# Taps and decays of a long convolution: four block buffers, loaded three blocks ahead

## The chip, the cores and the metric

One core of a Trainium2 chip. The metric is the time of one execution on the device in microseconds, the median of three runs. The core has TensorE (PE; its weight loads are shown as PEld), VectorE (DVE), ScalarE (ACT), GpSimd (POOL) and SyncE (SP), which run their own instruction streams and wait for each other by semaphores. Transfers are issued into queues by SP, ACT and POOL and carried by 16 DMA engines.

## What is computed

Two residual layers over x of shape 8 x 4096 x 512 in float32. The first is a layer norm, a causal convolution along the 4096 positions with a kernel of its own for each of the 512 channels (a sum of 16 decaying exponentials), and a scaled copy; the second is a mixture of 8 low-rank experts, of which each token takes two. Cut to the core:

```python
x = x + conv(layernorm(x))     # k[d,l] = sum_n p*beta*gamma*scale * q[d,n]**l, plus omega*input
x = x + experts(layernorm(x))  # y = w * (gelu(x @ A1.T @ B1) @ A2.T @ B2), for 4096 tokens
```

The experts' layer has as many tokens as one sequence has positions here (4096 of 32768), so it touches an eighth of the rows.

## The kernel before

The 4096 positions of a sequence are cut into 32 chunks of 128. A chunk's rows lie on the 128 partitions, 8 sequences x 32 chunks = 256 chunks lie along the free side. The work is done in two halves of four sequences (g = 0 and g = 1), and between them stands the experts' layer. I call g = 0 the first layer and g = 1 the last one, by their place in time.

A half is cut into four tiles of 128 channels (`DG` = 4, t = 0 to 7 over both halves), each of 128 x 128 x 128 floats, which is 8.39 MB; a tile into 8 blocks of 16 channels (`BT` = 8), and a block into two units of 8 channels. `xb` holds two tiles, one in each half of it: while tile t is computed in one, tile t-1 is stored from the other and then tile t+1 loaded into it. Each of these is cut into 16 pieces of 512 KB (`PIECES`).

The convolution inside a chunk is a product with a 128 x 128 Toeplitz matrix of taps for each channel; what goes from chunk to chunk is a scan. A unit is made of: centring by the mean, one half of the channels on POOL (L512) and the other on DVE (L1137); scaling on DVE (L1148); the chunks' sums into the states on PE (L1333, with `near`); the shift of the states on ACT (L859) and the scan on DVE (L1174); the local product on PE (L1346, with `wb`) and what the carried states add (L1358); and the addition to x on DVE (L1158).

The Toeplitz matrices of a block are made on chip from its taps. The taps (256 KB) and decays (128 KB) of all 32 blocks are written to HBM at the start and are then loaded, block by block, in both halves. `taps_in` holds the taps of two blocks, block i on partitions 32(i%2) to 32(i%2)+31. ACT turns them into `wb` (`reverse`, L878 and L879, two calls for a block) and copies half of the matrix (`lower`, L885). POOL copies the decays from `dk` to `near` (`place_decays`, L482). `wb` and `near` hold two blocks.

What sets the order of the transfers is SP's instruction stream. For each block of a tile (b = 0 to 7) `tile` issues `load_weights` for the next block (taps L683, decays L686), then at b = 0 waits until the tile before is wholly added (`s_ev`), and then issues its share of the 32 pieces, 4 or 5 in a step: first the 16 stores of tile t-1 (L638 and L641), then the 16 loads of tile t+1 (L618). A load of piece j waits for the store of that piece by a running count. The first tile of a half has nothing to store, the last nothing to load. `load_weights(i, h)` waits until the taps and decays of block i-2 have been turned and placed, and until all decays before have landed; all this is in SP's order, so that what stands behind a wait waits too. `centre` on POOL and DVE waits for all pieces of x of its tile (`s_x`).

The first two blocks are loaded from ACT's queue (L837, L838), while the rows of x stream in for the statistics. POOL's `centres` is written out in Python for g = 0 (all indices constants); for g = 1 it runs in a hardware loop with indices in registers, except at the first and last block of each tile.

Of the kernel before, what the change touches and what calls it, by code (L numbers as in the profile page):

```python
# [48 lines left out]
def build(nc, x, delta, alpha, beta, gamma, omega, ew, ei, w1a, w1b, w2a, w2b, out, ei_experts=8):  # L49
# [20 lines left out]
    TB = 4  # L70
    NL = P // LR
# [35 lines left out]
    with ctx:  # L107
# [17 lines left out]
        dk = sb("dk", [P, 2, N * KD])  # L125
# [125 lines left out]
        s_dk = sem("s_dk")  # L251
# [9 lines left out]
        s_w = [sem(f"s_wk{k}") for k in range(2)]  # L261
# [13 lines left out]
        s_out = sem("s_out")  # L275
        s_first = sem("s_first")
# [110 lines left out]
        def _(pool):  # L387
# [85 lines left out]
            def place_decays(i):  # L473

                h = i % 2
                if not isinstance(i, int):
                    h = pool.snap(h)
                dst = near[:, bass.ds(h, 1)].rearrange("p h s z n -> p (h s) z n")[:, :, 0:3:2, :]
                src = dk[:, bass.ds(h, 1)].rearrange("p h (n s d) -> p (h s) d n", s=SB, d=2)
# [22 lines left out]
            def centres(g):  # L502
                def centre(i, first, final):
                    for k in range(2):
                        u = 2 * i + k
                        if k == 0 and tile_start(i, g):
                            place_decays(i)
                        if not (g == 0 and isinstance(i, int) and i < BT):
                            wait(pool, s_x, tiles_in(i, g))
                        wait(pool, s_xn, u - 1)  # L510
                        wait(pool, s_st, u - 1)
                        pool.tensor_tensor(cen[:, k, 0:UC // 2].rearrange("p d r -> p r d"),  # L512
                                           unit_view(pool, g, i, k)[:, :, 0:UC // 2],
                                           mean[:, g * P:(g + 1) * P][:, :, None].to_broadcast([P, P, UC // 2]),
                                           ALU.subtract).then_inc(s_cen, 1)
                        if g == 1 and first and k == 0:
                            scatter(NQ - 1, 0)
                        if k == 0 and not tile_start(i, g) and not (g == 1 and first):
                            place_decays(i)
                        if g == 0 and first and k == 1:  # L520
                            clear(1)
                        if g == 0 and SENT + u < NSEND:
                            send(SENT + u)
                if g == 0:
                    for i in range(NK):
                        centre(i, i == 0, i == NK - 1)
                else:
                    over_tile_blocks(pool, g, lambda i, begin, end: centre(i, isinstance(i, int) and i == NK, end))
# [55 lines left out]
            pool.wait_ge(s_first, 16 * YP * DG)  # L584
# [19 lines left out]
        def _(sp):  # L604
# [18 lines left out]
            def stored(g, t):  # L623

                def until(j):
                    if g == 1:
                        return 0, 16 * (PIECES - YP) * (DG - 1) + 16 * PIECES * (t - DG) + 16 * (j + 1)
                    if j < YP:
                        return 16 * YP * t + 16 * (j + 1), 0
                    return 0, 16 * (PIECES - YP) * t + 16 * (j + 1 - YP)  # L630
                return until

            def store_tile(g, t, pieces):

                for j in pieces:
                    r0, row, d0 = piece(g, t, j)
                    if g == 0 and j < YP:
                        sp.dma_start(y_rows[:, j * PR:(j + 1) * PR, bass.ds(d0, P)],  # L638
                                     xb_row[:, bass.ds(r0, PR), :]).then_inc(s_first, 16)
                    else:  # L640
                        sp.dma_start(o_rows[:, bass.ds(row, PR), bass.ds(d0, P)],  # L641
                                     xb_row[:, bass.ds(r0, PR), :]).then_inc(s_out, 16)
# [29 lines left out]
            def load_weights(i, h):  # L672
# [10 lines left out]
                sp.dma_start(taps_in[h * ZR:(h + 1) * ZR], src).then_inc(s_w[h], 16)  # L683
                wait(sp, s_wd, placed)
                wait(sp, s_dk, kept)
                sp.dma_start(dk[:, h, :], dec).then_inc(s_dk, 16)  # L686

            def tile(g, t, first, final):
                for b in range(BT):
                    if not (first and b == 0) and not (final and b == BT - 1):  # L690
                        load_weights(t * BT + b + 1, (b + 1) % 2)
# [11 lines left out]
                    if final and g == 0 and b >= BT // 2:  # L703
                        if b == BT // 2:
                            sp.wait_ge(s_out, 16 * (PIECES - YP) * t)
                            sp.wait_ge(s_first, 16 * YP * t)
# [61 lines left out]
            load_weights(NK, 0)  # L768
            load_weights(NK + 1, 1)
# [11 lines left out]
            sp.wait_ge(s_out, 16 * (PIECES - YP) * (DG - 1) + 16 * PIECES * DG)  # L781

        @block.scalar
        def _(act):
# [48 lines left out]
            for h in range(2):  # L833
                row = taps_d[h:h + 1].rearrange("k s i d -> k (s i d)")
                src = bass.AP(row.tensor, row.offset, [[2, ZR], [2 * (P + ZR), SB], [1, 2 * P]])
                wait(act, s_dk, 16 * h)
                act.dma_start(taps_in[h * ZR:(h + 1) * ZR], src).then_inc(s_w[h], 16)  # L837
                act.dma_start(dk[:, h, :], decay_d[h:h + 1].rearrange("k s n d -> (k s) (n d)")).then_inc(s_dk, 16)  # L838
# [6 lines left out]
            def steps(i, h, first, final):  # L845
                for k in range(2):
# [18 lines left out]
                    if not final:  # L865
                        reverse(i + 1, k, 1 - h)
# [5 lines left out]
            def reverse(i, k, h):  # L872

                dst = wb[:, h, k * QB:(k + 1) * QB]
                src = taps_in[h * ZR:(h + 1) * ZR, k * QB:(k + 1) * QB].rearrange("p s (m d) -> p s d m", d=2)[:, :, :, ::-1]
                wait(act, s_w[h], 16 * (i // 2 + 1))
# [18 lines left out]
            def over_parities(g):  # L895
# [12 lines left out]
            over_parities(0)  # L908
# [63 lines left out]
            over_parities(1)  # L972
# [541 lines left out]
```

## Time and profile before

| | |
|---|---|
| median of three runs | 1257.15 us (1255.29 to 1258.32) |
| profiled execution | 1263.37 us, its span 1261.3 us |
| busy PE / DVE / ACT / POOL | 76% / 72% / 67% / 49% of the span |
| moved | 287.88 MB, 228 GB/s over the span |
| first half of the convolution (g = 0) | about 128 to 431 us |
| experts' layer | about 431 to 925 us |
| last half (g = 1) | about 925 to 1230 us, then its last stores |

The profile is of one execution. Its shares of busy time are means over stages that differ, so the stages are read one by one. A DMA share is the mean busy share of the 16 DMA engines, counted over their packets; it can be a little over 1. In a wait, "A <- B" says that A sat idle and that B released it; a wait for several things is put down to the one that came last. A "q" behind an engine (SPq) is its queue of transfers and registers.

### The profile page before, as it was taken

The numbers are of one execution on the slowest core, as the hardware profiler recorded it, in microseconds if no ns is written. First come the engines' busy times: TensorE is split into PE (matmuls) and PEld (weight loads), VectorE is DVE, ScalarE is ACT, GpSimd is POOL, SyncE is SP. The second block draws the span as 40 slices with busy tenths as digits, with TensorE's granted clock in tenths as the row PEclk, the third lists the DMA queues.
The fourth block names the chain that finished last, engine by engine and source line by source line (L and its number), as shares of the span: only waits on it lengthen the run. The fifth ranks groups of instructions, "written<-read, shape, count | busy, mean of one in ns | idle before, by whom it ended". The sixth has DMA issues, their size and how long they took to land.

```text
span 1261.3 us, 34527 instructions
## 1 busy us (share of the span) xinstructions
PE 954.1 (76%) x11452; PEld 770.1 (61%) x11452; DVE 909.8 (72%) x1495; ACT 842.9 (67%) x1191; POOL 617.4 (49%) x755
## 2 busy tenths in 40 slices
PE   3740787768778849999999899998978776776780
PEld 2520676656666736777777677776756665665660
DVE  6978898758769527777777777775469885775880
ACT  4841787758668726767766667667678776675870
POOL 4142886647545126666766666665553232231320
PEclk9975899889879969999999999999989898887995
DMA  7998957979979899999998898884368599898909
GB/s 247 326 387 293 226 132 207 273 178 288 272 193 282 275 280 278 261 252 267 238 226 232 200 226 229 228 200 107 82 155 187 141 286 233 228 267 182 283 17 266
DMA packets 337535, 287.88 MB, mean 228 GB/s; under 512 B 18088, under 2 KB 285000, under 8 KB 336962
## 3 DMA queue, kind: packets, MB, share of 16 engines
q1 hardware_dynamic: 293698, 212.01, 61.3%
q0 software_dynamic: 19520, 36.26, 14.7%
q10 hardware_dynamic: 24256, 38.81, 9.2%
q8 instruction: 37, 0.61, 0.2%
q14 instruction: 24, 0.20, 0.1%
HBM read 197.41 MB, written 100.61 MB: 236 GB/s over the span
## 4 chain that ended last, share of the span: by engine, by line
PE 27%; SPq 20%; DMA 12%; issue 11%; DVE 8%; ACT 2%; POOL 1%; POOLq 1%; DVEq 1%; ACTq 0%
SPq L641 8%; PE ps L1440 7%; DMA wide<-y_d,pick_g 7%; SPq L618 7%; PE ps L1453 6%; DMA wide<-taps_d 4%; PE ps L1346 3%; SPq L683 3%; DVE xb L1158 3%; PE ps L1358 2%; PE ps L1413 2%; PE ps L1465 2%; PE ps L1425 2%; PE ps L1333 2%; SPq L686 1%
## 5 line engine op out<-in xcount | busy, mean ns | idle before, releaser
L1346 PE MATMUL ps<-xn,wb 128*128 128x128 f32 x2048 | 294.1, 303 | 46.5 <-ACT wb L885 46.4
L1346 PEld LDWEIGHTS ps<-xn,wb 128*128 128x128 f32 x2048 | 268.1, 211 | 65.7 <-ACT wb L885 51.2
L512 POOL TENSOR_TENSOR cen<-xb,mean 128x512 f32<-128x512 f32 x128 | 142.2, 1111 | 270.3 <-DVE state L1174 218.5
L951 ACT ACTIVATE cen<-ps 128x1024 f32<-128x1024 f32 x156 | 155.9, 1021 | 136.5 <-PE ps L1440 120.4
L1148 DVE TENSOR_TENSOR xn<-cen,rstd 128x1024 f32<-128x1024 f32 x128 | 171.5, 1340 | 58.2 <-POOL cen L512 43.3
L878 ACT ACTIVATE wb<-wide 32x1024 f32<-32x1024 f32 x128 | 145.9, 1140 | 88.5 <-DMA wide<-taps_d 71.0
L1333 PE MATMUL ps<-xn,near 128*32 128x128 f32 x2048 | 89.8, 297 | 146.2 <-DVE xn L1148 75.4
L1440 PE MATMUL ps<-carry,wb 64*128 64x256 f32 x1248 | 169.9, 402 | 26.6 <-DVE carry L1221 26.3
L1158 DVE TENSOR_TENSOR xb<-xb,ps 128x1024 f32 (+1 forms) x128 | 152.8, 1194 | 14.0 <-PE ps L1358 13.8
L1453 PE MATMUL ps<-cen,xn 128*64 128x128 f32 x2496 | 161.1, 277 | 0.9 <-ACT cen L951 0.8
L1453 PEld LDWEIGHTS ps<-cen,xn 128*64 128x64 f32 x2496 | 136.7, 137 | 39.7 <-ACT cen L951 19.9
L1333 PEld LDWEIGHTS ps<-xn,near 128*32 128x32 f32 x2048 | 53.6, 115 | 170.0 <-issue 96.8
L493 POOL DMA_INDIRECT out<-carry,pick_s x78 | 126.4, 1621 | 56.0 <-issue 40.4
L1440 PEld LDWEIGHTS ps<-carry,wb 64*128 64x128 f32 x1248 | 113.6, 189 | 57.1 <-issue 44.7
L1137 DVE TENSOR_TENSOR cen<-xb,mean 128x512 f32<-128x512 f32 x128 | 137.5, 1074 | 0.0
L879 ACT ACTIVATE wb<-wide 32x768 f32<-32x768 f32 x128 | 116.3, 909 | 1.5
L1202 DVE BATCH_NORM_STATS2 tstat<-wide 128x6 f32<-128x512 f32 x78 | 53.7, 692 | 84.5 <-DMA wide<-y_d,pick_g 78.6
L561 POOL COPY xn<-xb 128x256 f32 x156 | 83.8, 583 | 58.3 <-PE ps L1453 57.3
L544 POOL DMA_INDIRECT wide<-y_d,pick_g x78 | 84.7, 1086 | 48.1 <-POOL pick_g L541 36.2
L459 POOL DMA_INDIRECT slot_d<-rowf,posi x64 | 100.3, 1567 | 11.0 <-issue 10.6
L1358 PE MATMUL ps<-state,carry 32*128 32x128 f32 x2048 | 96.9, 305 | 0.1
L1174 DVE TENSOR_TENSOR_SCAN state<-carry,shift_s 128x128 f32<-128x128 f32 x128 | 51.6, 403 | 60.0 <-ACT shift_s L859 59.8
(164 smaller groups left out, 1352.7 us busy)
## 6 DMA issues: line engine op xcount, KB each, us to landing
out<-xb SPq DMA_DIRECT2D x116, 512.0 KB
xb<-L_attn_x SPq DMA_DIRECT2D x96, 512.0 KB
xb<-L_attn_x SPq DMA_DIRECT2D x32, 1024.0 KB, 9.7
xb<-L_attn_x ACTq DMA_DIRECT2D x128, 256.0 KB
wb<-L_ffn_w_B SPq DMA_DIRECT2D x78, 256.0 KB
wide<-taps_d SPq DMA_DIRECT2D x62, 256.0 KB
y_d<-xb SPq DMA_DIRECT2D x16, 512.0 KB
dk<-decay_d SPq DMA_DIRECT2D x62, 128.0 KB
```

What stands on the lines that cost most here:

```text
L493: pool.indirect_dma_start(out=o_tok[0:T], out_offset=bass.IndirectOffsetOnAxis(ap=pick_s[:, 2 * k + h:2 * k + h + 1], axis=0), in_=route_o ...
L512: pool.tensor_tensor(cen[:, k, 0:UC // 2].rearrange("p d r -> p r d"), unit_view(pool, g, i, k)[:, :, 0:UC // 2], mean[:, g * P:(g + 1) * ...
L878: act.activation(dst[0:ZR], src, ACT.Copy)
L951: act.activation(act_h[:, b % 2].rearrange("p f t -> p (f t)"), ps[:, 2 * (b % 2):2 * (b % 2) + 2, :].rearrange("p a t -> p (a t)"), ACT.G ...
L1137: dve.tensor_tensor(cen[:, k, UC // 2:].rearrange("p d r -> p r d"), unit_view(dve, g, i, k)[:, :, UC // 2:], mean[:, g * P:(g + 1) * P][: ...
L1148: dve.tensor_tensor(xn[:, k], cen[:, k], rstd[:, g * P:(g + 1) * P][:, None, :].to_broadcast([P, UC, P]), ALU.mult).then_inc(s_xn, 1)
L1158: dve.tensor_tensor(view, view, ps[:, QB * k:QB * k + QB, 0:2 * P] .rearrange("p b (d r) -> p r b d", d=2), ALU.add).then_inc(s_ev, 1)
L1333: ins = pe.matmul(ps[b * 2 * N:(b + 1) * 2 * N, QB * k, 2 * P:3 * P], near[:, h, k * QB + b, d:d + 2, :].rearrange("p z n -> p (z n)"), xn ...
L1346: ins = pe.matmul(ps[:, QB * k + b, d * P:(d + 1) * P], wb[:, h, k * QB + b, d, :], xn[:, k, 2 * b + d, :], start=(b > 0 and d == 0), stop ...
L1358: ins = pe.matmul(ps[:, QB * k + b, d * P:(d + 1) * P], carry[rows, k, d * P:(d + 1) * P], state[rows, k, :], start=False, stop=True, skip ...
L1440: ins = pe.matmul(ps[:, 2 * (b % 2) + h, f * QT:(f + 1) * QT].rearrange("p (a t) -> p a t", a=2), w1bs[half_rows, k, c * P:(c + 1) * P], r ...
L1453: ins = pe.matmul(ps[h * RANK:(h + 1) * RANK, 4, 0:P], w2as[:, (f // 2) * (FC // 2) + 2 * b + f % 2, :], act_h[:, b % 2, f, h * P:(h + 1) ...
```

## The change

- `dk` and `taps_in` hold four blocks (`WB` = 4), the taps of block i on partitions 32(i%4) to 32(i%4)+31. `wb` and `near` still hold two.
- In step b of a tile SP loads block b+3 instead of b+1. Each buffer of `dk` has a semaphore of its own, and the wait for all decays before is gone. The last tile of a half issues loads in its first five steps only.
- At the start ACT's queue loads four blocks instead of two, and before the last half SP loads four. ACT's loop runs over four blocks (`over_quarters`), because the buffer's number must be a constant.
- Each of the 16 pieces has a semaphore for its stores (`s_put`), in place of two running counts.
- `centres` on POOL is written out for g = 1 too, because `place_decays` now takes constant indices only.

```diff
-        dk = sb("dk", [P, 2, N * KD])
+        dk = sb("dk", [P, WB, N * KD])
@@ place_decays
-                wait(pool, s_dk, 16 * (i + 1))
+                wait(pool, s_dk[i % WB], 16 * (i // WB + 1))
@@ centres
-                if g == 0:
-                    for i in range(NK):
-                        centre(i, i == 0, i == NK - 1)
-                else:
-                    over_tile_blocks(pool, g, lambda i, begin, end: centre(i, isinstance(i, int) and i == NK, end))
+                for i in range(g * NK, (g + 1) * NK):
+                    centre(i, i == g * NK, i == (g + 1) * NK - 1)
@@ load_tile
-                        y_done, o_done = stored(j)
-                        wait(sp, s_first, y_done)
-                        wait(sp, s_out, o_done)
+                        wait(sp, s_put[j], 16 * stored(j))
@@ load_weights
-                turned, placed = 2 * (i - 1), i - 1
-                kept = 16 * i
-                now(sp, turned, placed, kept)
+                turned, placed = 2 * (i - WB + 1), i - WB + 1
+                now(sp, turned, placed)
                 wait(sp, s_rev, turned)
-                sp.dma_start(taps_in[h * ZR:(h + 1) * ZR], src).then_inc(s_w[h], 16)
+                sp.dma_start(taps_in[k * ZR:(k + 1) * ZR], src).then_inc(s_w[k], 16)
                 wait(sp, s_wd, placed)
-                wait(sp, s_dk, kept)
-                sp.dma_start(dk[:, h, :], dec).then_inc(s_dk, 16)
+                sp.dma_start(dk[:, k, :], dec).then_inc(s_dk[k], 16)
@@ tile
-                    if not (first and b == 0) and not (final and b == BT - 1):
-                        load_weights(t * BT + b + 1, (b + 1) % 2)
+                    if not (first and b == 0) and not (final and b + WB > BT):
+                        load_weights(t * BT + b + WB - 1, (b + WB - 1) % WB)
@@ before the last half
-            load_weights(NK, 0)
-            load_weights(NK + 1, 1)
+            for k in range(WB):
+                load_weights(NK + k, k)
@@ ACT, first loads
-            for h in range(2):
+            for k in range(WB):
...
-                wait(act, s_dk, 16 * h)
@@ ACT, loop
-                with act.Fori(g * NK // 2, (g + 1) * NK // 2 - 1) as p:
-                    steps(p * 2 + 1, 1, False, False)
-                    steps(p * 2 + 2, 0, False, False)
-                steps((g + 1) * NK - 1, 1, False, True)
+                with act.Fori(g * NK // WB, (g + 1) * NK // WB - 1) as p:
+                    for m in range(1, WB + 1):
+                        steps(p * WB + m, m % WB, False, False)
+                for m in range(1, WB):
+                    steps((g + 1) * NK - WB + m, m, False, m == WB - 1)
```

## Rows read from the trace of the kernel before

**Rows 1.** Waits of the whole run: engine, line, releaser: us in total, times, longest.

```profile
POOL near L482 <- DMA dk<-decay_d: 43.7, 13, 6.9
ACT wb L878 <- DMA wide<-taps_d: 71.0, 28, 5.2
...
SPq L618 <- DMA out<-xb: 0.3, 2, 0.2
```

**Rows 2.** Timeline of SP: start, duration in us, issues merged, each tile's first store.

```profile
196.83 4.03 SPq L638 DMA_DIRECT2D y_d<-xb  x4
...
231.65 1.95 SPq L683 DMA_DIRECT2D wide<-taps_d  x1
...
264.75 1.24 SPq L683 DMA_DIRECT2D wide<-taps_d  x1
...
280.48 4.01 SPq L638 DMA_DIRECT2D y_d<-xb  x4
...
362.37 4.00 SPq L638 DMA_DIRECT2D y_d<-xb  x4
...
430.65 4.12 SPq L638 DMA_DIRECT2D y_d<-xb  x4
...
995.18 3.97 SPq L641 DMA_DIRECT2D out<-xb  x4
...
1078.33 3.96 SPq L641 DMA_DIRECT2D out<-xb  x4
...
1160.91 3.94 SPq L641 DMA_DIRECT2D out<-xb  x4
...
1229.71 26.26 SPq L641 DMA_DIRECT2D out<-xb  x16
```

**Rows 3.** Windows of 10 us: busy time by engine, granted clock, DMA share, GB/s.

```profile
80.00:90.00 10.00, 0.41 (x5) 0.17 (x2) 7.42 (x12) 1.18 (x3) 4.84 (x7) 0.71 1.06 401
90.00:100.00 10.00, 0.00 (x0) 0.00 (x0) 6.79 (x12) 1.20 (x2) 4.70 (x6) 0.50 1.07 333
290.00:300.00 10.00, 7.24 (x116) 6.05 (x116) 9.19 (x11) 8.31 (x12) 8.09 (x7) 1.00 1.08 291
340.00:350.00 10.00, 6.34 (x68) 5.34 (x72) 5.02 (x6) 6.88 (x10) 3.95 (x5) 0.68 1.19 278
```

**Rows 4.** Windows of 2 us behind the last transfers of two long tiles.

```profile
272.00:274.00 2.00, 0.39 (x16) 0.19 (x8) 0.00 (x0) 1.96 (x3) 1.55 (x2) 1.00 0.20 54
1152.00:1154.00 2.00, 0.63 (x16) 0.44 (x16) 0.00 (x0) 1.52 (x2) 0.82 (x2) 1.00 0.23 46
```

**Rows 5.** Chain that ended last, in order of time: start, us, what; two places.

```profile
192.44 1.98 PE ps L1346 x16
...
334.86 7.34 DMA wide<-taps_d
...
344.96 3.78 PE ps L1346 x16
```

**Rows 6.** Timeline of ACT in the tile from 280: turning of taps.

```profile
289.01 0.91 ACT L879 ACTIVATE wb<-wide 32x768 f32<-32x768 f32 x1
...
342.22 1.12 ACT L878 ACTIVATE wb<-wide 32x1024 f32<-32x1024 f32 x1 [4.11 <-DMA wide<-taps_d]
```

**Rows 7.** Waits of ACT for taps, 362 to 431 us and 1161 to 1230 us.

```profile
ACT wb L878 <- DMA wide<-taps_d: 2.7, 2, 1.4
...
ACT wb L878 <- DMA wide<-taps_d: 1.5, 2, 0.8
```

**Rows 8.** Timeline of DVE in the first tile of either half: scaling of units.

```profile
155.91 1.23 DVE L1148 TENSOR_TENSOR xn<-cen,rstd 128x1024 f32<-128x1024 f32 x1 [0.24 <-POOL cen L512]
...
163.85 1.22 DVE L1148 TENSOR_TENSOR xn<-cen,rstd 128x1024 f32<-128x1024 f32 x1 [0.24 <-POOL cen L512]
...
970.15 1.22 DVE L1148 TENSOR_TENSOR xn<-cen,rstd 128x1024 f32<-128x1024 f32 x1 [0.38 <-POOL cen L512]
...
978.36 1.22 DVE L1148 TENSOR_TENSOR xn<-cen,rstd 128x1024 f32<-128x1024 f32 x1 [0.38 <-POOL cen L512]
```

More of the change, by code:

```diff
@@ L70, in build @@
     TB = 4
+    WB = 4
     NL = P // LR
@@ L250, in build @@
         s_tapd = [sem(f"s_tapd{k}") for k in range(TB)]
-        s_dk = sem("s_dk")
+        s_dk = [sem(f"s_dk{k}") for k in range(WB)]
         s_wd = sem("s_wd")
@@ L260, in build @@
         s_x = sem("s_x")
-        s_w = [sem(f"s_wk{k}") for k in range(2)]
+        s_w = [sem(f"s_wk{k}") for k in range(WB)]
         s_cen = sem("s_cen")
@@ L274, in build @@
         s_ev = sem("s_ev")
-        s_out = sem("s_out")
-        s_first = sem("s_first")
+        s_put = [sem(f"s_put{k}") for k in range(PIECES)]
         s_wl1 = sem("s_wl1")
@@ L473, in place_decays @@
             def place_decays(i):
[L475 to L479, printed above, removed]
+                dst = near[:, i % 2][:, :, 0:3:2, :]
+                src = dk[:, i % WB].rearrange("p (n s d) -> p s d n", s=SB, d=2)
                 wait(pool, s_loc, 2 * (i - 1))
-                wait(pool, s_dk, 16 * (i + 1))
+                wait(pool, s_dk[i % WB], 16 * (i // WB + 1))
                 pool.tensor_copy(dst, src).then_inc(s_wd, 1)
@@ L583, in _ @@
             pool.wait_ge(s_sf, 4)
-            pool.wait_ge(s_first, 16 * YP * DG)
+            for j in range(YP):
+                pool.wait_ge(s_put[j], 16 * DG)
             pool.wait_ge(s_yz, 16)
@@ L623, in stored @@
             def stored(g, t):
[L625 to L631, printed above, removed]
+                return lambda j: t + 1 if g == 0 or j < YP else t
             def store_tile(g, t, pieces):
@@ L637, in store_tile @@
                     if g == 0 and j < YP:
[L638 to L642 removed]
+                        dst = y_rows[:, j * PR:(j + 1) * PR, bass.ds(d0, P)]
+                    else:
+                        dst = o_rows[:, bass.ds(row, PR), bass.ds(d0, P)]
+                    sp.dma_start(dst, xb_row[:, bass.ds(r0, PR), :]).then_inc(s_put[j], 16)
             for j, a in enumerate((delta, alpha, beta)):
@@ L670, in _, with load_weights @@
             sp.wait_ge(s_keep, NL)
-            def load_weights(i, h):
+            def load_weights(i, k):
                 kb = i % NK if isinstance(i, int) else sp.snap(i % NK)
@@ L704, in tile @@
                         if b == BT // 2:
-                            sp.wait_ge(s_out, 16 * (PIECES - YP) * t)
-                            sp.wait_ge(s_first, 16 * YP * t)
+                            for j in range(PIECES):
+                                sp.wait_ge(s_put[j], 16 * t)
                         j = b - BT // 2
@@ L780, in _ @@
             sp.wait_ge(s_outb, 16 * PIECES)
-            sp.wait_ge(s_out, 16 * (PIECES - YP) * (DG - 1) + 16 * PIECES * DG)
+            for j in range(PIECES):
+                sp.wait_ge(s_put[j], 16 * (NT if j < YP else NT - 1))
         @block.scalar
@@ L843, in deviations, with steps @@
                                bias=eps[:, 0:1]).then_inc(s_std, 1)
-            def steps(i, h, first, final):
+            def steps(i, m, first, final):
+                h = m % 2
                 for k in range(2):
@@ L865, in steps @@
                     if not final:
-                        reverse(i + 1, k, 1 - h)
+                        reverse(i + 1, k, (m + 1) % WB)
                     if k == 0:
@@ L870, in steps, with reverse @@
                         lower(i + 1, 0, 1 - h)
[L872 to L876, printed above, removed]
+            def reverse(i, k, m):
+                dst = wb[:, m % 2, k * QB:(k + 1) * QB]
+                src = taps_in[m * ZR:(m + 1) * ZR, k * QB:(k + 1) * QB].rearrange("p s (m d) -> p s d m", d=2)[:, :, :, ::-1]
+                wait(act, s_w[m], 16 * (i // WB + 1))
                 wait(act, s_loc, 2 * (i - 1))
@@ L907, in _ @@
             act.wait_ge(s_rt, NROUTE)
-            over_parities(0)
+            over_quarters(0)
             def weights_out(n0, n1):
@@ L971, in _ @@
                 act.wait_ge(s_s[2 + h], 16 * (NQ // 2))
-            over_parities(1)
+            over_quarters(1)
         @block.vector
```

8 lines of the change are left out of this document (4 added, 4 removed).

## The prediction

> **What bounds the kernel now.** I read the views in this order: the waits of the whole run, the transfer queue's own timeline, the busy windows, the chain of waits, and then ScalarE and VectorE close up. The waits show what the change aims at: ScalarE's turning of the taps waits 71.0 us in 28 places for a taps load, and GpSimd's placing of the decays waits 43.7 us in 13 places for a decay load [rows 1]. The two overlap, since they wait for neighbouring transfers of the same queue, so they are not added.
>
> The timeline of SP, the engine that issues those loads, shows the frame in which they sit. The first store of a tile can be issued only when the last addition of that tile is done, so its start marks the end of a tile. Call the marks S0 to S3 in the first layer (196.83, 280.48, 362.37, 430.65) and S4 to S7 in the last (995.18, 1078.33, 1160.91, 1229.71) [rows 2]. The tiles between them take 83.65, 81.89 and 68.28 us, then 83.15, 82.58 and 68.80 us. The two short ones are the last tiles of their layers: beside them run 16 stores and no loads of x. The four long ones have 16 stores and 16 loads beside them.
>
> The windows say why the long ones are long. A long tile moves 8.39 MB out and 8.39 MB in (128 x 128 x 128 floats each) and eight sets of taps and decays of 0.39 MB, 19.9 MB in all. While that runs, the DMA engines are full: share 1.08 at 291 GB/s in the stores, 1.19 at 278 GB/s in the loads [rows 3]. But they don't run to the end of the tile. The transfer engines fall quiet about 272, 352, 1068 and 1152 us (the windows of the first and the last of the four stand in the rows, with shares of 0.20 and 0.23) [rows 4], that is 75.2, 71.5, 72.8 and 73.7 us after the tile's first store. The last 9 to 10 us of each long tile are compute that came late, with an idle queue.
>
> Why it came late, the chain shows in one place: the taps issued at 334.86 land 7.34 us later, behind pieces of x that were queued before them [rows 5]. ScalarE idles 4.11 us for them and turns them from 342.22 on [rows 6], and then TensorE's 16 matmuls follow. The buffers of two blocks make a loop of it: turn block i-1, free its buffer, issue block i+1 behind some 2 MB, wait, turn. So a long tile is neither pure compute nor pure transfer, but each waits for the other in turn.
>
> **The change, part by part.**
>
> *Four buffers, loads three blocks ahead.* In the step of block b, SP loads block b+3 instead of b+1. What it waits for is the same: the turning of block b-1 and the placing of its decays (2(i-1) with i=b+1, against 2(i-3) with i=b+3). The number of loads, their bytes and their place among the pieces of x are the same too; the block that they carry is needed two blocks, 16 us, later. The tightest case is the eighth block of a tile, which SP now issues in step 4: 231.65 in a tile that began at 196.83 [rows 2], so 34.8 us in, and landed about 42.2 us in (plus the 7.34). ScalarE wants it while it works on the seventh block, some 6 x 8.0 = 48 us in. Margin 6 us: the taps waits inside a tile should be gone, and with them those of the decays, whose load follows at once.
>
> What is late next, once they are gone? Compute needs its own 8 blocks; the transfers need their 19.9 MB. Compute alone (C): the last tile of the first layer, less its remaining taps waits, 68.28 - 2.7 = 65.6 us; the last tile of the last layer 68.80 - 1.5 = 67.3 us [rows 7]. Transfers alone (D): from the first store to the quiet 71.5 to 75.2 us, mean 73.3. Where the queue is never empty, the ramp at its start goes (about 2 us), and by the rate it is 19.9 MB at 285 GB/s, the mean of the two windows, = 70 us. I take 71, with 69 to 74 as bounds. D is larger than C, so the middle tiles go at the pace of the queue: the stores of tile t are issued while the last loads of tile t+1 still move, and compute waits at the tile's edge for its x instead of waiting inside for taps.
>
> First layer, from S0: the loads of tile 2 land at 73.3; compute of tile 1 is done at 66 and waits. The loads of tile 3 land 71 later, at 144.3. Tile 3 then takes 65.6, so S3 comes 209.9 after S0, where it now comes at 233.8. Gain 23.9. Last layer, from S4: 73.3 + 71 + 65.5 (C of the next part) = 209.8 against 234.5. Gain 24.7.
>
> *GpSimd's centring of the last layer, written out instead of looped.* Here VectorE is on the chain: it waits for GpSimd's half of the centring 0.24 us in each unit of the first layer, where the code was already written out, and 0.38 in the last, where GpSimd computes its wait values in registers between the scan and its own start. The same block takes 163.85 - 155.91 = 7.94 us there and 978.36 - 970.15 = 8.21 us here [rows 8]. So 0.27 us for each of the looped blocks, at most 7 of a tile: 1.8 us. That counts in the first tile of the last layer (1.8) and in its last one (67.3 - 1.8 = 65.5, used above), and not in the two that go at the queue's pace. From below it is 0, if VectorE's own loop is what costs.
>
> *ScalarE's loop of four blocks.* The same activations and as many waits; a jump back every 32 us instead of every 16. Nothing, within 0.5 us either way.
>
> *A semaphore for each store piece.* A load of piece j waits for the store of piece j alone. SP waited 0.3 us in all for this [rows 1], since 15 issues, some 30 us, lie between the two while a transfer lands in 7. Nothing. The decay loads no longer wait for the decays before them; that wait stood where SP had time, beside compute. Behind SP's waits are queued the pieces of x, so what goes from it goes to the queue; at a tile that is bound by bytes it is worth nothing.
>
> *Two more sets of taps and decays at the start.* ScalarE's queue issues four pairs instead of two near 90 us, in the stretch in which the rows of x stream in. That stretch is full: 401 GB/s from 80 to 90 us, and 333 from 90 to 100 with two pairs in it [rows 3]. In those 10 us x lost 4.0 - (3.3 - 0.8) = 1.5 MB, or 3.7 us. Two more pairs take about as much, part of which VectorE catches up by itself: 0 to 4 us of loss, I take 3. At the start of the last layer two more pairs go while the queue is nearly empty: nothing.
>
> Sum: -23.9 - 24.7 - 1.8 + 3 = -47 us. The profiled execution took 1263.37 us (span 1261.3), so it would take 1216. It lies 6.2 above the median 1257.15; the median would become 1257.15 - 47 = 1210, and with the edges of the tiles not quite seamless I leave it there, at 1210.
>
> **The rivals.**
>
> *The queue runs dry on the turning of taps.* Compute of a middle tile now starts when its x lands, some 8 us after SP began on the tile's steps, and SP still may not issue step b before block b-1 is turned. The steps come some 8.7 us apart (four of them in the 34.8 us above), so SP reaches step 2 some 17 us into its tile, which begins about 268 (the last taps of the tile before go out at 264.75, and one pair follows) [rows 2]: at 285. Compute starts at 196.8 + 73.3 = 270, and the turning that step 2 needs is done 9.4 us after the tile's start (289.93 in the tile that began at 280.48) [rows 6]: at 280. That leaves 5 us to spare, a little more with every step. If that margin fails, or the reads and writes hinder each other more at the seams, each of the four long tiles ends some 5 us later: gain 27, 1230 us. For it: 5 us is thin. Against it: the queue holds 7 us of work when SP pauses.
>
> *It hardly matters.* If the taps come late because the whole queue is slow, and compute stretches with the transfers whatever the order (D 80 rather than 71), the four long tiles stay at about 80: gain 8, less 3 at the start, 1252 us; with a little less, no change. Against it: the quiet 9 to 10 us at the end of each long tile [rows 4].
>
> *TensorE's clock, slower than before.* The new wait at the tile's edge is one of 8 us in which TensorE has nothing. Sixteen matmuls of the local product take 1.98 us at full clock and 3.78 us at half [rows 5]. At half clock the three groups of a unit take about 6.3 us instead of a pitch of 4.0. Should the clock stay at half through the tile behind such a wait, 16 units x 2.3 = 37 us are lost in each of the four tiles behind one, 147 in all: 1357 us. It decides from about a third of the units, where the loss of 12 us a tile eats the gain. Against it: the present kernel has such a pause at each tile's edge too, and ten microseconds behind the one at 280 the granted clock is 1.00 [rows 3]; the half clock comes back only with the taps waits (0.68 from 340 to 350), which go.
>
> The Trainium skill, "TensorE: Matmul & The Clock Gate", section "HAM oscillation — how this bites in real kernels", tells of just this pattern: a matmul phase behind each DMA wait starts at the lower rate, every time. By that rule alone each long tile would begin with a stretch at 1.2 GHz; the trace agrees that it does, but it does so now as well, so C already has it.
>
> **How the numbers follow.** Forecast 0.76 (1210, from 1198 with D at 69, nothing lost at the start and a little from the pacing, to 1222 with D at 74 and 4 lost). Queue runs dry 0.13 (1230). Hardly matters 0.06 (1245 to 1257, a third of it within 0.2% of before). Clock 0.02, and 0.01 for slower in another way. A rest of 0.02 faster than 1198. The range 1197 to 1228 takes in the forecast and about half of the first rival. A difference of 0.2% (2.5 us) is about what a measurement of this kernel can tell from no change. Faster 0.93, same 0.04, slower 0.03.
>
> **What would show it.** Right: the middle tiles of both layers take 70 to 74 us instead of 82 to 84, the last ones 66; ScalarE's waits for taps fall from 71 us to under 10; the DMA share stays at 1 across the edges of the middle tiles; waits for x appear at the edges, 5 to 9 us each, on GpSimd or VectorE. The pitch of a block in the last layer is 7.9 instead of 8.2. Wrong: taps waits that remain in the fifth to eighth block (the margin of 6 us), SP waits for ScalarE in the middle tiles with a share under 1 (first rival), a middle tile at 80 with a full queue (second), a granted clock of 0.5 long after a tile's edge (third), or a first layer that begins more than 4 us later.

## The result, and the profile after

The changed kernel takes 1225.67 us (1217.28 to 1229.09, 4 runs) against 1256.22 us (1254.27 to 1258.32, 4 runs): ratio 0.9747, 95% interval 0.9694 to 0.9799. Forecast were 1210 us, with 1197 to 1228 as range: the sign and the place are right, but 47 us were promised and 31 came, and the time lies 2 us inside the slow end of the range. The profiled execution took 1217.28 us, span 1215.3. It is the fastest of the four, so the terms below are read from this profile and two more of the same kernel.

The timeline of SP answers to [rows 2]; columns as there, each line a tile's first store.

```profile
201.05 4.02 SPq L628 DMA_DIRECT2D y_d<-xb  x4
...
272.48 5.90 SPq L628 DMA_DIRECT2D y_d<-xb  x4
...
344.64 5.83 SPq L628 DMA_DIRECT2D y_d<-xb  x4
...
415.93 4.16 SPq L628 DMA_DIRECT2D y_d<-xb  x4
...
971.72 3.97 SPq L628 DMA_DIRECT2D out<-xb  x4
...
1041.53 6.29 SPq L628 DMA_DIRECT2D out<-xb  x4
...
1113.75 5.45 SPq L628 DMA_DIRECT2D out<-xb  x4
...
1183.76 26.31 SPq L628 DMA_DIRECT2D out<-xb  x16
```

The long tiles, 82 to 84 us before, are 70 to 72 now, and their queue is never idle at an edge. The last tiles of the two halves, 68.3 and 68.8 us before, have become longer, 71.3 and 70.0; the prediction had 66 for them. A mark of a middle tile now tells less than it did: its first store may be issued while compute already waits. What ends a middle tile is seen on GpSimd, in the first centring behind each edge (in brackets its idle time and what ended it):

```profile
274.28 1.83 POOL L509 TENSOR_TENSOR cen<-xb,mean 128x512 f32<-128x512 f32 x1 [12.51 <-DMA xb<-L_attn_x]
...
346.48 1.83 POOL L509 TENSOR_TENSOR cen<-xb,mean 128x512 f32<-128x512 f32 x1 [8.71 <-DMA xb<-L_attn_x]
...
1044.21 2.89 POOL L509 TENSOR_TENSOR cen<-xb,mean 128x512 f32<-128x512 f32 x2 [13.32 <-DMA xb<-L_attn_x]
...
1114.52 2.89 POOL L509 TENSOR_TENSOR cen<-xb,mean 128x512 f32<-128x512 f32 x2 [8.77 <-DMA xb<-L_attn_x]
```

All four edges behind a long tile wait for x: GpSimd 8.7 to 13.3 us, and VectorE, which has work up to the edge, 0.8 to 5.6 us (13.4 in all four). ScalarE's waits for taps, 71.0 us in 28 places before, are one wait at the very start. In the kernel before, the wait there lasted 15.9 us and was put down to a decay load, so it isn't among the 71.0. Waits of the whole run:

```profile
POOL cen L509 <- DMA xb<-L_attn_x: 82.6, 23, 13.3
...
ACT wb L863 <- DMA wide<-taps_d: 13.9, 1, 13.9
```

The windows across the edge at 274 show what happens there: the DMA share stays over 1, TensorE is at 2.43 of 10 us and its granted clock at 0.52, and both are back in the window that begins 20 us later. Between 201 and 345 us SP never waits for ScalarE or for GpSimd.

```profile
260.00:270.00 10.00, 7.08 (x112) 5.97 (x106) 5.92 (x6) 7.23 (x11) 1.74 (x2) 1.00 1.15 266
270.00:280.00 10.00, 2.43 (x22) 2.02 (x23) 4.71 (x4) 1.17 (x2) 5.39 (x4) 0.52 1.09 293
280.00:290.00 10.00, 7.64 (x96) 6.42 (x95) 8.31 (x11) 7.83 (x12) 6.73 (x6) 0.84 1.08 310
290.00:300.00 10.00, 8.77 (x119) 7.66 (x122) 8.20 (x10) 8.76 (x13) 7.11 (x7) 0.95 1.01 283
```

Where the time went, from SP's marks in each profile: start (to the first store of tile 1), first half (from it to the first store behind the last tile), experts (to the first load of taps for the last half), first tile of the last half, last half, final stores. All in us.

| profile | start | first half | experts | first tile | last half | stores | span |
|---|---|---|---|---|---|---|---|
| before | 196.8 | 233.8 | 478.3 | 86.2 | 234.5 | 31.6 | 1261.3 |
| before_again | 195.6 | 233.4 | 479.4 | 86.7 | 228.4 | 31.6 | 1255.1 |
| after | 201.1 | 214.9 | 471.1 | 84.7 | 212.0 | 31.5 | 1215.3 |
| after_again | 202.1 | 215.7 | 479.7 | 84.8 | 212.6 | 31.6 | 1226.3 |
| after_third | 200.4 | 216.4 | 476.3 | 84.7 | 215.3 | 31.6 | 1224.6 |

The means differ by +5.0 (start), -18.0 (first half), -3.2 (experts), -1.7 (first tile), -18.2 (last half), 0 (stores): -36. The medians of the runs differ by 31. The forecast had +3, -23.9, 0, -1.8 and -24.7.

### The profile page after: what moved, and what is told of

It is laid out like the page before. It is cut to its first block and busy times, and to the rows that moved or that the text cites. A ratio compares the mean times of both kernels' runs of the same rounds, so it can differ in the third digit from the quotient of the medians.

```text
span 1215.3 us, 34118 instructions
## 1 busy us (share of the span) xinstructions
PE 924.6 (76%) x11452; PEld 747.5 (62%) x11452; DVE 914.0 (75%) x1495; ACT 850.7 (70%) x1191; POOL 628.5 (52%) x755
## 3 DMA queue, kind: packets, MB, share of 16 engines
q0 software_dynamic: 19520, 36.26, 15.1%
## 5 line engine op out<-in xcount | busy, mean ns | idle before, releaser
L509 POOL TENSOR_TENSOR cen<-xb,mean 128x512 f32<-128x512 f32 x128 | 145.1, 1135 | 264.5 <-DVE state L1160 176.9
L1332 PE MATMUL ps<-xn,wb 128*128 128x128 f32 x2048 | 276.6, 291 | 0.0
L1332 PEld LDWEIGHTS ps<-xn,wb 128*128 128x128 f32 x2048 | 251.8, 201 | 17.8 <-issue 3.7
L1134 DVE TENSOR_TENSOR xn<-cen,rstd 128x1024 f32<-128x1024 f32 x128 | 176.4, 1378 | 49.8 <-POOL cen L509 43.6
L1426 PE MATMUL ps<-carry,wb 64*128 64x256 f32 x1248 | 166.4, 395 | 26.7 <-DVE carry L1207 26.5
L1439 PEld LDWEIGHTS ps<-cen,xn 128*64 128x64 f32 x2496 | 136.4, 137 | 38.6 <-ACT cen L937 31.6
L1123 DVE TENSOR_TENSOR cen<-xb,mean 128x512 f32<-128x512 f32 x128 | 139.5, 1090 | 13.5 <-DMA xb<-L_attn_x 13.4
L459 POOL DMA_INDIRECT slot_d<-rowf,posi x64 | 106.1, 1658 | 10.7 <-issue 9.8
L538 POOL DMA_INDIRECT wide<-y_d,pick_g x78 | 84.7, 1085 | 48.1 <-POOL pick_g L535 36.1
L844 ACT ACTIVATE shift_s<-ps,coef 128x124 f32<-128x124 f32 x128 | 46.5, 363 | 86.2 <-PE ps L1319 83.5
```

The source lines that it names most:

```text
L1123: dve.tensor_tensor(cen[:, k, UC // 2:].rearrange("p d r -> p r d"), unit_view(dve, g, i, k)[:, :, UC // 2:], mean[:, g * P:(g + 1) * P][: ...
L1134: dve.tensor_tensor(xn[:, k], cen[:, k], rstd[:, g * P:(g + 1) * P][:, None, :].to_broadcast([P, UC, P]), ALU.mult).then_inc(s_xn, 1)
L1332: ins = pe.matmul(ps[:, QB * k + b, d * P:(d + 1) * P], wb[:, h, k * QB + b, d, :], xn[:, k, 2 * b + d, :], start=(b > 0 and d == 0), stop ...
L1426: ins = pe.matmul(ps[:, 2 * (b % 2) + h, f * QT:(f + 1) * QT].rearrange("p (a t) -> p a t", a=2), w1bs[half_rows, k, c * P:(c + 1) * P], r ...
L1439: ins = pe.matmul(ps[h * RANK:(h + 1) * RANK, 4, 0:P], w2as[:, (f // 2) * (FC // 2) + 2 * b + f % 2, :], act_h[:, b % 2, f, h * P:(h + 1) ...
```

## The experiments

**Where an execution's scatter lies.** The kernel before and the changed one once more, unedited; the changed one twice.

> The changed kernel as it is, once more. Theory A (the middle tiles go at the pace of the transfer queue, and the rest is as measured): its single times lay between 1217 and 1229 us, so the median should be 1222 to 1228, and the tiles again take 72, 70 to 72 and 69 us in both halves; the time by which one execution differs from another should lie outside the convolution. Rival B (the scatter lies in the queue's pace in the middle tiles): a profile with another time would show middle tiles longer or shorter by that difference, divided among four.

> The kernel before, once more, for a second profile of it beside that of the changed kernel on the same chip. Theory A (the scatter of an execution lies in the experts' layer): the first half from the first store 233 to 235 us, the last 233 to 235, and what is left of the difference to the first profile (span 1261.3) in the experts' layer. Rival B (the convolution itself scatters by 5 us or more): one of the halves outside 232 to 236.

> The changed kernel, a third profile. Theory A: first half from the first store 214 to 216 us, last half 212 to 213, the experts' layer anything from 471 to 480 (from the first store behind the first half to the first load of taps ahead of the last half). Rival B: as for the kernel before.

Measured: after_again 1225.27 us (1217.52 to 1231.27, 6 runs), ratio 0.9759 (0.9728 to 0.979), which repeats the result. The experts' layer scatters most, 471 to 480 us, and both kernels have values near 479: the first profile of the changed kernel had a short one, and 7 of its 46 us are from there. But the convolution scatters too. The last half was 234.5 in the first profile of before and 228.4 in the second, in which one of its long tiles took 78.4 us instead of 82.6; after the change it was 212.0 to 215.3. So rival B of before_again holds for that half, and theory A is too simple. The prediction was made against a profile whose last half was 3 us longer than the mean of the two.

**The distance alone.** The changed kernel with all its semaphores, buffers and loops, but each block loaded one ahead again, and two pairs instead of four loaded at the start of each half.

```diff
-                    if not (first and b == 0) and not (final and b + WB > BT):
-                        load_weights(t * BT + b + WB - 1, (b + WB - 1) % WB)
+                    if not (first and b == 0) and not (final and b + 1 == BT):
+                        load_weights(t * BT + b + 1, (b + 1) % WB)
...
-                turned, placed = 2 * (i - WB + 1), i - WB + 1
+                turned, placed = 2 * (i - 1), i - 1
```

> The changed kernel, with everything it brings (four buffers, semaphores by piece, both loops), but with each block's taps and decays loaded one block ahead, as before the change, and two pairs loaded at the start of each half. Theory A (the distance is the whole gain): the waits for taps come back, the long tiles take 80 to 84 us again, 1250 to 1256 us. Rival B (a good part comes from the semaphores by piece or the decay wait that is gone): 1230 to 1245 us.

Measured: 1253.62 us (12 runs), ratio to before 0.998 (0.9954 to 1.0005). In its profile the waits for taps are back (86.7 us, 30 times; 13.5 of it the one at the start), and the long tiles with them:

```profile
ACT wb L863 <- DMA wide<-taps_d: 86.7, 30, 13.5
```

```profile
194.38 4.02 SPq L628 DMA_DIRECT2D y_d<-xb  x4
...
279.02 4.01 SPq L628 DMA_DIRECT2D y_d<-xb  x4
...
361.42 4.00 SPq L628 DMA_DIRECT2D y_d<-xb  x4
```

84.6 and 82.4 us. The distance is the gain, as theory A had it; the semaphores by piece, the missing wait on earlier decays and the loops are together worth 3 us, by the interval something between none and 6.

**How far is enough.** The same with two blocks ahead (`b + WB - 2`, the waits of SP moved along, and three pairs loaded at the start of each half).

> The changed kernel, but loading two blocks ahead instead of three (the same four buffers, the same waits of SP, three pairs loaded ahead). Theory A (taps are wanted some 48 us into a tile in the eighth block and are there by 42 with three blocks ahead, so one block of 8 us less puts them 2 us late at the end of a tile and about in time before): ScalarE waits for taps by 2 to 4 us in the last blocks of the four long tiles; but since the queue sets the pace of the two middle tiles of a half, little of it is seen in the time: 0 to 4 us slower than the changed kernel. Rival B (the depth of three is what matters, and with two most of the old waits come back): 15 to 25 us slower than the changed kernel.

Measured: 1225.74 us (6 runs), ratio 0.9774 (0.9748 to 0.98), against 1225.27 with three ahead. Apart from the wait at the start ScalarE waits twice, 5 us in all:

```profile
ACT wb L863 <- DMA wide<-taps_d: 19.3, 3, 14.2
```

The two waits are 3.3 us at the end of the first long tile of the first half and 1.8 at that of the last half; theory A, which had such waits in all four long tiles, holds for the time. The third block of distance is worth nothing that can be measured here. The comparison isn't of distance alone: with three pairs instead of four the first store of tile 1 comes at 199.2 instead of 201.2 (mean of three), and the halves, 216.1 and 215.7 us, are at the upper end of the changed kernel's (214.9 to 216.4 and 212.0 to 215.3).

**GpSimd's loop alone.** The kernel before, with `centres` written out for the last half (two lines in `place_decays` that only the loop needs are gone too).

```diff
-                if g == 0:
-                    for i in range(NK):
-                        centre(i, i == 0, i == NK - 1)
-                else:
-                    over_tile_blocks(pool, g, lambda i, begin, end: centre(i, isinstance(i, int) and i == NK, end))
+                for i in range(g * NK, (g + 1) * NK):
+                    centre(i, i == g * NK, i == (g + 1) * NK - 1)
```

> The kernel before, with GpSimd's centring of the last half written out and nothing else changed. Theory A (0.27 us a block where compute is on the chain, that is in the first and the last tile of the last half, and a little in the long ones between their waits for taps): 3.5 to 6 us faster than before, a pitch of 7.94 instead of 8.21 us. Rival B (VectorE's own loop is what costs): no difference, within 1 us, and a pitch of 8.2.

Measured: 1256.19 us (12 runs), ratio 1.0007 (0.9984 to 1.0029). The timeline of VectorE answers to [rows 8]:

```profile
952.02 1.23 DVE L1143 TENSOR_TENSOR xn<-cen,rstd 128x1024 f32<-128x1024 f32 x1 [0.27 <-POOL cen L510]
...
960.01 1.22 DVE L1143 TENSOR_TENSOR xn<-cen,rstd 128x1024 f32<-128x1024 f32 x1 [0.27 <-POOL cen L510]
```

The block takes 7.99 us instead of 8.21 and the wait is 0.27 instead of 0.38, so the mechanism is shown, and the loop on VectorE isn't the cause. The first tile takes 84.7 us as in the changed kernel (86.2 and 86.7 before), the last 67.6 instead of 68.8. That is 3 us, the interval of the ratio reaches to 2.0 us of gain, and the median shows none: what it brings in time stays open, and neither theory's time is shown.

**The start.** The changed kernel, third and fourth pairs loaded by SP behind the rows of x.

```diff
-            for k in range(WB):
+            for k in range(2):
                 row = taps_d[k:k + 1].rearrange("k s i d -> k (s i d)")
...
+            sp.wait_ge(s_w[0], 16)
+            for k in range(2, WB):
+                load_weights(k, k)
             tiles(0)
```

> The changed kernel, with only two pairs of taps and decays loaded from ScalarE's queue at the start; the third and fourth are loaded by SP after the rows of x, ahead of the first tile. Theory A (two more pairs cost the first half's start 4 us, because the stretch from 80 to 120 us is full): the first store of tile 1 comes at 197 instead of 201, and the time falls by 3 to 5 us against the changed kernel. Rival B (the later start is scatter or has another cause): no difference, within 1 us.

Measured: 1221.18 us (1221.01 to 1222.69, 5 runs), ratio 0.9735 (0.9715 to 0.9754), 4.1 under the changed kernel on the same chip; the intervals overlap. The first store of tile 1 is where theory A puts it:

```profile
196.40 3.96 SPq L628 DMA_DIRECT2D y_d<-xb  x4
```

In the changed kernel the windows that answer to [rows 3] have 284 and 310 GB/s, where the kernel before has 333 and 363:

```profile
90.00:100.00 10.00, 0.00 (x0) 0.00 (x0) 5.79 (x10) 5.20 (x6) 3.95 (x5) 0.50 1.08 284
100.00:110.00 10.00, 0.00 (x0) 0.00 (x0) 4.46 (x9) 0.95 (x2) 1.23 (x2) 0.50 1.07 310
```

From 90 to 120 us the rate is 326 against 345 GB/s, 0.6 MB less in all, and the two added pairs are 0.8 MB of what moves. So 1.4 MB of x come later, which is 3.4 us at 401 GB/s.

**Queue or compute.** First, 128 KB of taps for a block instead of 256. The taps of half the channels are then stale, so this kernel leaves out part of the convolution.

```diff
-                src = bass.AP(row.tensor, row.offset, [[2, ZR], [2 * (P + ZR), SB], [1, 2 * P]])
-                sp.dma_start(taps_in[k * ZR:(k + 1) * ZR], src).then_inc(s_w[k], 16)
+                src = bass.AP(row.tensor, row.offset, [[2, ZR], [2 * (P + ZR), SB // 2], [1, 2 * P]])
+                sp.dma_start(taps_in[k * ZR:(k + 1) * ZR, 0:SB // 2], src).then_inc(s_w[k], 16)
```

> The changed kernel with 128 KB of taps for each block that SP loads instead of 256 KB; the taps of the other half of the channels are stale, so this half of the convolution's product is left out. 1 MB less goes through the queue in each long tile, 3.7 us at 285 GB/s. Theory A (the queue sets the pace of the middle tiles): the loads of tiles 2 and 3 land 3.7 and 7.4 us earlier after the first store, and the last tile of each half ends 5 to 7.5 us earlier: 11 to 15 us faster than the changed kernel. Theory C (queue and compute are now about level: compute takes 70 us from the landing of x to the end of the tile, the queue 70 to 72): the first landing of a half counts in full, the second only until compute is the later one: 4 to 6 us for each half, 8 to 12 in all, and the waits for x at the second edge go nearly to zero. Rival B (compute alone sets the pace): under 3 us.

Measured: 1207.88 us (6 runs), 17.4 under the changed kernel. The halves take 207.3 and 206.6 us, 8.4 and 6.7 less than the means of the three profiles above; the rest is in the other stages. GpSimd at the first edge, then SP's marks:

```profile
270.91 1.83 POOL L509 TENSOR_TENSOR cen<-xb,mean 128x512 f32<-128x512 f32 x1 [9.40 <-DMA xb<-L_attn_x]
```

```profile
200.81 4.02 SPq L628 DMA_DIRECT2D y_d<-xb  x4
...
340.56 4.10 SPq L628 DMA_DIRECT2D y_d<-xb  x4
...
408.07 4.17 SPq L628 DMA_DIRECT2D y_d<-xb  x4
```

x lands 70.1 us behind the first store (73.2 in the changed kernel), tile 2 takes 69.7 from there, and then the last tile 67.5 with no wait for x at its edge. The queue counts at the first edge and compute is the later one at the second: theory C by its mechanism. Its size, 8 to 12 us, was too small: the two halves gain 15.1 in the profile and the median 17.4, above the 11 to 15 of theory A as well. Of the halves' excess, 2 us each are that a last tile that doesn't wait at its edge is 2 us shorter; the rest of the 17.4 isn't explained.

Second, half of each store piece of the output, so that only compute is left in the tiles; half of those output rows are never written.

```diff
-                        dst = o_rows[:, bass.ds(row, PR), bass.ds(d0, P)]
-                    sp.dma_start(dst, xb_row[:, bass.ds(r0, PR), :]).then_inc(s_put[j], 16)
+                        dst = o_rows[:, bass.ds(row, PR // 2), bass.ds(d0, P)]
+                    n = PR if g == 0 and j < YP else PR // 2
+                    sp.dma_start(dst, xb_row[:, bass.ds(r0, n), :]).then_inc(s_put[j], 16)
```

> The changed kernel, storing only the first half of the rows of each piece of the output (the pieces that feed the experts' layer are stored whole). The queue carries 3.1 to 4.2 MB less in each long tile, 11 to 15 us, so that it can't be what the middle tiles wait for, and the last store takes 13 us less. What is left in the tiles is compute. Theory C: all six tiles behind the first stores take 67 to 69 us, no waits for x at the edges, 204 us in the first half from the first store to the last (215 in the changed kernel) and 203 in the last one (212): 20 us, and 13 at the end, 33 faster. By the prediction's 65.6 us of compute it would be 197 and 196, 45 faster.

Measured: 1183.55 us (4 runs). The marks of the first half:

```profile
199.17 4.03 SPq L629 DMA_DIRECT2D y_d<-xb  x4
...
266.93 4.01 SPq L629 DMA_DIRECT2D y_d<-xb  x4
...
334.52 4.01 SPq L629 DMA_DIRECT2D y_d<-xb  x4
...
402.05 4.18 SPq L629 DMA_DIRECT2D y_d<-xb  x4
```

67.8, 67.6 and 67.5 us, and 67.4 or 67.5 for each tile of the last half, whose sum is 202.4. VectorE waits for x at none of the edges. Compute by itself takes 67.5 us a tile, not 65.6. It is the tiles that say so: the time, 42 us under the changed kernel, lies between the 33 of theory C and the 45 that 65.6 would give.

**A better order.** On top of late_pairs, the taps and decays of step 6 go behind that step's pieces of x, and in a second kernel those of step 5 as well (`b in (5, 6)`).

```diff
+                    ahead = not (first and b == 0) and not (final and b + WB > BT)
+                    behind = b == 6 and not first
-                    if not (first and b == 0) and not (final and b + WB > BT):
+                    if ahead and not behind:
                         load_weights(t * BT + b + WB - 1, (b + WB - 1) % WB)
...
                             load_tile(g, t + 1, [j - PIECES], stored(g, t - 1))
+                    if ahead and behind:
+                        load_weights(t * BT + b + WB - 1, (b + WB - 1) % WB)
```

> The kernel with the third and fourth pairs loaded by SP at the start (1221 us, 4 faster than the changed kernel), and with the taps and decays of step 6 of a tile issued behind the pieces of x of that step instead of ahead of them. They are needed two blocks later, and x, which compute waits for at the tile's edge, lands one pair earlier, 1.4 us. Theory A (x at the edge is on the path): the first edge of each half comes 1.4 us earlier, the second as well where the queue is the later one: 1.5 to 3 us faster than without this edit. Rival B (compute is level with the queue and takes it up, or the taps are then late): within 1.5 us of it.

> Third and fourth pairs by SP at the start as in behind_x, and the taps and decays of steps 5 and 6 behind those steps' pieces of x. Those of step 5 are turned for the first block of the next tile, just ahead of the edge. Theory A (x at the edge is on the path): nothing more from step 5, since only what is put behind the last piece of x lets x land earlier, and the step's own pieces stand ahead of step 6 anyway: within 2 us of behind_x (1215). Rival B (the first block's taps come late at the edge): 2 to 6 us slower than behind_x, with waits for taps at the edges.

Measured: behind_x 1215.22 us (1210.66 to 1224.17, 6 runs), ratio to before 0.9676 (0.9638 to 0.9715), 10 under the changed kernel and 6 under late_pairs, where 1.5 to 3 were expected. Against late_pairs (0.9715 to 0.9754) the intervals just meet, so this step isn't shown in time. The first landing of x comes 70.9 us behind the first store (at 195.83), where late_pairs has 73.5, and in the last half 70.5 where it has 73.0; here GpSimd at the first edge in behind_x:

```profile
266.75 1.83 POOL L509 TENSOR_TENSOR cen<-xb,mean 128x512 f32<-128x512 f32 x1 [10.20 <-DMA xb<-L_attn_x]
```

The halves take 214.3 and 211.4 us, 1.4 and 1.7 less than in late_pairs: 3 of the 6 us. The other 3 lie in the experts' layer (475.1 and 477.9), which scatters by more than that. behind_two 1217.10 us (6 runs), ratio 0.9669 (0.9637 to 0.9702): the same, as theory A had it. Both beat the changed kernel clear of noise, by the later pairs and the order together.

## Why the prediction was right, and what it mis-sized

**The loop of two buffers** was the cause, and the distance ended it (one_ahead). The margin of 6 us at three blocks was real, and larger than needed: two blocks do. No taps wait is left inside a tile.

**What is late next** was named right: x at the tile's edge, with a full queue. The landings behind the first store, 73.0 us in the mean of six (three profiles, both halves), were forecast at 73.3. The second landing follows 72.1 behind the first in the mean, where 71 were taken: 1.1 us too little in each half.

**Compute, 65.6 us, is the term that failed.** From the landing to the end the last tile takes 69.4 us in the mean of six, 3.8 more than forecast. There are two parts. First, the prediction took ScalarE's waits of 2.7 and 1.5 us in the last tiles [rows 7] off the tile's time, as if a wait anywhere were time on the path. half_stores has 67.5 us with none of these waits, and pool_only has the same 67.5 in the last tile of its first half with 2.2 us of them (waits of ScalarE there, 362 to 431 us):

```profile
ACT wb L873 <- DMA wide<-taps_d: 2.2, 2, 1.2
```

one_ahead has 67.5 and 67.4 with 2.0 and 2.1 us. So only 0.8 of the 2.7 us was on the path (68.3 less 67.5), and of the 1.5 nothing. This part is 1.9 us of the 3.8.

Second, a tile that waits for its x starts later after the landing than a tile that finds it there after its edge. The timeline of VectorE behind the landing at 274:

```profile
274.23 1.04 DVE L1123 TENSOR_TENSOR cen<-xb,mean 128x512 f32<-128x512 f32 x1 [5.60 <-DMA xb<-L_attn_x]
...
276.24 1.28 DVE L1134 TENSOR_TENSOR xn<-cen,rstd 128x1024 f32<-128x1024 f32 x1 [0.98 <-POOL cen L509]
277.44 1.95 DVE L1123 TENSOR_TENSOR cen<-xb,mean 128x512 f32<-128x512 f32 x1
279.48 1.23 DVE L1134 TENSOR_TENSOR xn<-cen,rstd 128x1024 f32<-128x1024 f32 x1
...
285.97 1.19 DVE L1144 TENSOR_TENSOR xb<-xb,ps 128x1024 f32<-128x1024 f32 x1
```

and of the kernel before at the edge of 280:

```profile
280.19 1.03 DVE L1137 TENSOR_TENSOR cen<-xb,mean 128x512 f32<-128x512 f32 x1
281.31 1.23 DVE L1148 TENSOR_TENSOR xn<-cen,rstd 128x1024 f32<-128x1024 f32 x1
282.45 1.05 DVE L1137 TENSOR_TENSOR cen<-xb,mean 128x512 f32<-128x512 f32 x1
283.60 1.23 DVE L1148 TENSOR_TENSOR xn<-cen,rstd 128x1024 f32<-128x1024 f32 x1
...
290.07 1.21 DVE L1158 TENSOR_TENSOR xb<-xb,ps 128x1024 f32<-128x1024 f32 x1
```

From the first centring to the first addition it is 11.7 us instead of 9.9. Before, GpSimd had done its centrings ahead of the edge, since x was there; now it starts together with VectorE, VectorE waits 0.98 us for it, and the next centring takes 1.95 us beside GpSimd's instead of 1.05. The whole 1.8 us is there already at the second scaling (279.48 - 274.23 = 5.25 us against 283.60 - 280.19 = 3.41), so TensorE, whose clock is low here, adds nothing to it.

**The start** was forecast at +3 and came at +5 in the profiles; late_pairs takes it back, 4 in the medians, though there the intervals overlap. The mechanism, bytes in a full stretch, fits (3.4 us by the windows above), and the loss was avoidable. A first half that begins more than 4 us later was one of the prediction's own signs of being wrong, and it came.

**GpSimd written out**: the first tile of the last half gained 1.7 us, where 1.8 was forecast. In the last tile pool_only gained 1.2 (68.8 to 67.6), not 1.8; with the 1.5 us of waits wrongly taken off, that is why 67.3 - 1.8 = 65.5 was forecast and 67.5 is measured.

**The reference.** The sum was made against a profile whose last half was 234.5 us; the second one had 228.4.

Summed by halves, with the means: landing 73.0, second 72.1, last tile 69.4 make 214.5 us. The forecast was 209.9 and 209.8, so 4.6 us are missing in each half, 2 at the start, and 3 from the reference: 14 us. Against that the experts' layer came out 3 us shorter in these profiles, which leaves -36 for -47, as the table has it. That the medians differ by 31 and the profiles by 36 stays open; it is within what the experts' layer scatters by (9 us), and what makes it scatter wasn't tried.

**Luck in the range.** The time fell inside 1197 to 1228, but neither of its ends was set for the term that failed: the slow end stands for transfers of 74 us and 4 us of start, and compute was given no bounds. The width meant for the queue happened to cover compute. Two smaller slips changed nothing in the sum: long tiles of 80 us would be 331.3 - 320 = 11 us of gain, not the 8 of the second rival, and the quiet ends of the long tiles are 8.5 to 10.4 us.

**The rivals.** The queue doesn't run dry: the DMA share is 1.01 or more across the edge at 274, and SP waits for ScalarE nowhere in the middle tiles of either half. "It hardly matters" is out with tiles of 70 to 72 us. The granted clock does fall at each landing, to 0.52 in the window from 270 to 280 (the kernel before has 0.83 there and from 280 to 290), and is at 0.95 in the window from 290; the first addition comes no later by it (above). The rule of the Trainium skill that the prediction cites, "TensorE: Matmul & The Clock Gate", section "HAM oscillation — how this bites in real kernels", describes a start at the lower rate behind each wait, and the trace agrees (0.52 at the edge); it changed nothing of the sum.

## What to carry to other kernels

When a small load stands in one queue with large ones, ask for two numbers: how long it lies behind them (7.3 us here) and how many steps ahead its buffer lets it be issued. Here a step is 8 us, one step ahead was too little and two were enough; all that a further one was seen to bring is one more pair of loads in the full stretch at the start. Before taking a wait off a stage's time, look for a run or a stretch without it, for an engine's wait for one thing is often covered by another's chain. When a queue and compute come out level (70 to 72 against 67.5 us), the edge between them is the next cost: try putting what is not urgent behind the last piece that compute waits for. Here x landed 2.5 us earlier by it, and its worth in time is not clear of noise.

## What the runs showed of the hardware

GpSimd's and VectorE's centring hinder each other when they start together. At the landing GpSimd's takes 1.83 us instead of 1.10 while VectorE's (1.04 us) runs beside it, and the next VectorE one 1.95 instead of 1.05 while GpSimd's second one runs (at 277.29, 1.19 us, so they share 1.04 us). The excesses are 0.73 and 0.90 us. The addition to x, which reads one operand from PSUM, isn't hindered: it takes 1.19 us at 285.97, and GpSimd's centring beside it, at 286.23, takes 1.09. The Trainium skill, "SBUF — State Buffer", section "SBUF: two separate sides", says that the two engines share a pair of ports, and that a VectorE operation with two inputs in SBUF and a GpSimd operation that reads SBUF exclude each other: one has the pair for its whole instruction and the other fully blocks. The rows agree in which operations are hindered; the excesses are somewhat shorter than the 1.04 us that a full block would give. In the steady part of a tile VectorE centres while GpSimd waits for the scan, so the centrings don't meet there.

The transfer queue keeps its pace across a tile's edge: 266, 293, 310 and 283 GB/s in the four windows above, though TensorE is busy for only 2.43 of 10 us in the second of them.
